# Two matmul layers of a dense FFN, dealt out in turns on TensorE: a quarter of the next unit's first layer, then one token tile of this unit's second layer

## The reference

```
x = x + L0_xattn(layernorm(x), ctx)
x = x + L0_ffn(layernorm(x))          # 8 experts, 2 per token
x = x + L1_xattn(layernorm(x), ctx)
x = x + L1_ffn(layernorm(x))          # 64 experts of 64, 8 per token, and 2 shared MLPs of 512
```

```
probs = softmax(xf @ router_w + router_b); tw, ti = top_k(probs, 8); tw = tw / sum(tw)
for e in range(64):
    h = silu(xf @ W1[e] + B1[e]) @ W2[e] + B2[e]
    acc = acc + (sum of tw where ti == e)[:, None] * h
shared = sum over 2 of (silu(xf @ SW1 + SB1) @ SW2 + SB2)
out = acc + shared
```

## Time and profile before

| | |
|---|---|
| time, median of 3 runs | 1457.45 us (1457.34 to 1457.92) |
| profiled execution: its time, its span | 1458.33 us, 1456.6 us |
| PE busy | 1396.3 us (96%) |
| PE weight loads busy | 1115.3 us (77%) |
| DVE busy | 1011.6 us (69%) |
| ACT busy | 779.7 us (54%) |
| POOL busy | 288.1 us (20%) |
| mean granted TensorE clock | 0.989 |
| stage D | from about 992 us to the end |

### The profile page before, as it was taken

How to read it: one execution, slowest core, us unless ns; L and a number is a source line. 1 busy time by engine, 2 the same in 40 slices (tenths; PEclk the granted TensorE clock), 3 DMA queues, 4 the chain that set the end, 5 groups by cost and what they waited for, 6 DMA issues and landing times.

```text
span 1456.6 us, 27434 instructions
## 1 busy us (share of the span) xinstructions
PE 1396.3 (96%) x9946; PEld 1115.3 (77%) x9946; DVE 1011.6 (69%) x2461; ACT 779.7 (54%) x1682; POOL 288.1 (20%) x329
## 2 busy tenths in 40 slices
PE   6999998998999979999999999999999999999998
PEld 5898997885556656666667666767899999999997
DVE  6767773565656668977877787776587776677753
ACT  4556663344766657777878777772443222222221
POOL 0000001243155232300000000002233332233321
PEclk9999999999999999999999999999999999999999
DMA  9432201423455111100000000001036544555441
GB/s 345 148 110 68 77 22 30 146 80 117 153 185 182 58 52 31 38 13 2 16 23 20 13 30 2 2 2 64 0 92 150 121 116 103 127 118 123 99 104 52
DMA packets 78479, 117.80 MB, mean 81 GB/s; under 512 B 7487, under 2 KB 51845, under 8 KB 77829
## 3 DMA queue, kind: packets, MB, share of 16 engines
q1 hardware_dynamic: 75269, 107.59, 25.7%
q0 software_dynamic: 3072, 8.39, 1.8%
HBM read 97.09 MB, written 18.87 MB: 80 GB/s over the span
## 4 chain that ended last, share of the span: by engine, by line
PE 81%; DVE 10%; issue 3%; ACT 3%; POOL 2%; DMA 1%; SPq 0%; ACTq 0%; DVEq 0%; POOLq 0%
PE PS L68 17%; PE PS L70 16%; PE PS L69 16%; PE PS L2602 7%; PE PS L2574 6%; PE PS L1292 5%; PE PS L2589 3%; PE PS L2617 3%; PE PS L1308 2%; PE PS L1186 2%; DVE a_pt L838 2%; DVE c_sm L2826 1%; POOL zs L1506 1%; DVE a_c L754 1%; ACT c_pr L2698 1%
## 5 line engine op out<-in xcount | busy, mean ns | idle before, releaser
L1842 ACT ACTIVATE d_hf<-PS,C 128x512 f32<-128x512 f32 x160 | 108.7, 691 | 255.0 <-PE PS L70 252.3
L953 POOL CAST d_h<-d_hf 128x512 fp32r<-128x512 f32 x160 | 126.2, 802 | 329.1 <-DVE d_hf L2050 248.3
L2707 ACT ACTIVATE c_pt<-PS 100x512 f32<-100x512 f32 x256 | 139.0, 595 | 93.7 <-PE PS L2589 93.5
L68 PE MATMUL PS<-d_w,d_h 128*128 128x256 f32 x640 | 182.2, 285 | 2.0 <-issue 1.4
L70 PE MATMUL PS<-d_w,d_h 128*128 128x256 f32 x640 | 179.8, 281 | 0.0
L69 PE MATMUL PS<-d_w,d_h 128*128 128x256 f32 x640 | 179.7, 281 | 0.0
L2698 ACT ACTIVATE c_pr<-c_sm,c_mn 128x400 f32<-128x400 f32 x256 | 158.7, 626 | 14.5 <-DVE c_mn L2826 14.5
L2826 DVE CUSTOM_DVE_ANT_0 c_sm<-PS,c_mw 128x400 f32<-128x400 f32 x256 | 136.0, 569 | 16.9 <-PE PS L2574 14.9
L958 DVE TENSOR_TENSOR d_h<-d_hf,d_h 128x512 fp32r<-128x512 f32 x160 | 129.7, 868 | 16.2 <-POOL d_h L953 13.2
L2050 DVE TENSOR_TENSOR d_hf<-d_hf,d_wb 128x512 f32<-128x512 f32 x128 | 89.8, 709 | 71.0 <-ACT d_hf L1842 70.6
L68 PE MATMUL PS<-ZT,d_w 128*128 128x512 f32 x320 | 126.1, 394 | 0.7 <-issue 0.7
(11 more groups left out here) (305 smaller groups left out, 3128.6 us busy)
## 6 DMA issues: line engine op xcount, KB each, us to landing
d_wb<-wscratch SPq DMA_DIRECT2D x64, 512.0 KB, 7.3
a_cT<-ctxT SPq DMA_DIRECT2D x4, 1601.0 KB, 7.7
a_raw_nat<-ctx SPq DMA_DIRECT2D x4, 1536.0 KB
zs<-e_zero SPq DMA_DIRECT2D x2, 2944.0 KB, 18.6
ys<-e_y SPq DMA_DIRECT2D x46, 128.0 KB, 1.8
d_w1r<-l_w SPq DMA_DIRECT2D x10, 512.0 KB, 4.0
d_w2r<-l_w SPq DMA_DIRECT2D x10, 512.0 KB, 5.2
e_z<-zs SPq DMA_DIRECT2D x9, 512.0 KB, 3.9
```

The costliest lines, as they stand in the source:

```text
L68: pe.matmul(out, w[0], x[0], start=first, stop=False)
L953: i = eng.tensor_copy(mem["h"][b % 2][0][:, m, :], mem["hf"][:, m, :])
L1842: act.activation(memD["hf"][:, m, :], PS[:, m, :], ACT.Silu, bias=C[:, b1 + m:b1 + m + 1]).then_inc(DM["act"], 1)
L2707: act.activation(c_pt[u % 2][0:KW, :, :, i * P + r * DH:i * P + (r + 1) * DH].rearrange("p h t q -> p (h t) q"), PS[0:KW, BT + r, :].rearr ...
```

## The change

Two code pieces change, both in `d_pe`. `second` now takes one tile `i`; its waits for `h_lo` and the rest stand ahead of tile 0, and its wait for `x_done` is halved: tile 0 waits for the first addition of the unit before (bank 4), tile 2 for the second (bank 5). The loop deals out quarters and tiles in turns. Nothing else of the program differs, and the number of instructions is the same.

```diff
-            def second(u):
+            def second(u, i):
                 g, b = u // B, u % B
-                pe.wait_ge(DM["h_lo"], u * 4 + 4)
...
-                wait_past(pe, x_done[3], u * 2)
...
+                if i == 0:
+                    pe.wait_ge(DM["h_lo"], u * 4 + 4)
...
+                if i % 2 == 0:
+                    wait_past(pe, x_done[3], (u - 1) * 2 + i // 2 + 1)
+                o = PS[:, 4 + i // 2, (i % 2) * D:(i % 2 + 1) * D]
+                for k in range(4):
+                    last = split_matmul(pe, o, [h[:, k, i * P:(i + 1) * P] for h in memD["h"][b % 2]],
+                                        [w[:, k, :] for w in memD["w2"][g % 2]], k == 0, k == 3 and g < GD - 1)
...
+                if i == QT - 1:
+                    last.then_inc(DM["y"], 1)
...
             for u in range(DU):
                 if u + 1 < DU:
-                    d_hidden(pe, u + 1)
-                second(u)
+                    d_hidden(pe, u + 1, [0])
+                for i in range(QT):
+                    second(u, i)
+                    if i + 1 < QT and u + 1 < DU:
+                        d_hidden(pe, u + 1, [i + 1])
```

More of the change, by code:

```diff
@@ L1881, in d_pe @@
         def d_pe(pe):
-            def second(u):
+            def second(u, i):
                 g, b = u // B, u % B
-                pe.wait_ge(DM["h_lo"], u * 4 + 4)
-                if u == 0:
-                    pe.wait_ge(DM["w_lo"], 2)
-                    pe.wait_ge(attn_done, 1)
-                wait_past(pe, x_done[3], u * 2)
-                if g == GD - 1:
[L1890 to L1900, removed]
+                if i == 0:
+                    pe.wait_ge(DM["h_lo"], u * 4 + 4)
+                    if u == 0:
+                        pe.wait_ge(DM["w_lo"], 2)
+                        pe.wait_ge(attn_done, 1)
+                    if g == GD - 1:
+                        pe.wait_ge(DR["one"], B)
+                        pe.wait_ge(DR["wt_out"], b + 1)
+                        pe.wait_ge(DR["w_in"], 64)
+                if i % 2 == 0:
[4 more added lines that the diff above has]
+                                        [w[:, k, :] for w in memD["w2"][g % 2]], k == 0, k == 3 and g < GD - 1)
+                if g == GD - 1:
+                    last = pe.matmul(o, d_wT[b][:, i * P:(i + 1) * P], d_b2[:, :], start=False, stop=True)
+                if i == QT - 1:
+                    last.then_inc(DM["y"], 1)
             def logits(b):
```

## The result

The change makes the kernel slower by 7%: 1559.06 us (median of 4, 1556.56 to 1561.84) against 1457.68 us (median of 4), ratio 1.0704, 95% interval 1.0691 to 1.0718, or 101.4 us. The prediction was 1568 us, with a range of 1538 to 1597. The kernel before took 1457.5 us in some groups of runs and 1489 to 1493 us in others, so each experiment is told by its distance from the kernel before of its own group; one run of the third experiment, over 1.5% above the fastest of its kernel, is left out of its figures.

What follows compares the result with a forecast made beforehand. TensorE was taken to bound stage D. Waits of 81.3 us, 85.4 with the opening, plus 25 us of clock falls made 110 us on the profiled 1458.33; less 0.9 for the median, 1568 us, range 1538 to 1597.

Steps and rivals of the forecast that it cites:

- What bounds the kernel: Stage D: TensorE sets the time, busy 244.40 of 244.40 us, with idle spots of only 0.55 and 1.43 us.
- The wait for the low parts: Ahead of tile 0 in each unit: a chain of 5.18 us against a cover of 2.78, so TensorE 2.4 us late.
- Units that round weights: Seven of units 8 to 36: low parts take 3.75 instead of 2.90 us beside GpSimd's cast, late by 3.25 us.
- Units 0 to 7: First units, without a multiply: 3.05 us against a cover of 2.78 plus router matmuls; nothing taken, bound 2 us.
- Opening: Start of stage D: three quarters of unit 1 no longer fill the wait for unit 0's low parts, 4.1 us lost.
- End: Last group: units 37 and 38 late by 2.0 us each, unit 39 by 3.3, net 1.7.
- Sum of the waits: Units 8 to 39 lose 81.3 us in waits, 85.4 us with the opening.
- Matmuls in turns: Borders between quarters and tiles on TensorE: cost and gain nil, bound 0.1 us per unit, 4 us in all.
- The clock: TensorE's clock behind the new pauses: 16 falls to the lower level at 1.56 us each, 25 us.
- at this length it is even odds: New pauses, some 2.15 us idle: the clock falls behind half of them, judged from six earlier stretches.
- the rival of 1544 us: Clock holds at pauses of 2.15 us and falls at the opening alone: 1544 us, chance 0.22.
- the upper one: Clock falls at nearly every pause, or the chain is longer than priced: 1591 us or above 1597, chance 0.17.

Runs made afterwards that it cites:

- the third experiment: The change, but tile 0 waits for both additions of the unit before, as in the kernel before: 1643.23 us against 1492.53 for the kernel before.
- the fifth experiment: The change, with GpSimd's cast of the next group's second-layer weights put between its casts of quarters 0 and 1: 1579.63 us against 1488.86 for the kernel before.
- the second run: The change itself measured once more, unaltered, in another group of runs: 1591.86 us against 1488.86 for the kernel before, ratio 1.0681.
- the sixth experiment: The change, with nine unread matmuls of 512 columns ahead of tile 0 in units 12 to 35: 1585.99 us against 1488.86 for the kernel before.

## Why the prediction was right

- **What bounds the kernel** stood: TensorE waited for nothing in D, and with the cover restored (8.5, 5.5 us) or turns limited to units 0 to 7 (6.0 us) it is back near the old time. No gain from turns was found.
- **The wait for the low parts**: 2.4 us late per unit was forecast, shown as a pause of 2.15; it is 2.22, and the period 13.62 (forecast 13.5). The parts of the chain were tested apart: low parts behind the fourth multiply (2.22 to 1.20 when two are moved away), the addition (2.22 to 2.81 with a second one), the cover (2.22 to nothing with 5.56 us), and that the pause has a fixed end (filled for nothing).
- **Units that round weights**: 3.06 us for a forecast of 3.0, in the six from 13 to 33; unit 9 has 2.62 and unit 8 1.78, since router matmuls stand in the cover, which I counted for units 0 to 7 and not for these (read from the code's order; no run moved them). That it is GpSimd's cast was shown by the fifth experiment.
- **Units 0 to 7**: nil, as taken. **Opening**: the 4.04 us pause against 0.55 before, 3.5 for a forecast of 4.1. **End**: 1.78 for units 37 and 38, 3.17 for unit 39 against 1.43, net 1.74 for a forecast of 1.7.
- **Sum of the waits**: 85.4 us forecast; 78.1 shown and 8 hidden are 86.
- **Matmuls in turns**: nil was taken. The period of 13.62 us is the 11.12 of before, the pause of 2.22 with 0.26 for its start and end, and 0.02 left over.
- **The clock** is the term that was off. Sixteen falls at 1.56 us were forecast, 25 us; there were nine, 14 us (the price of one held: periods with a fall are 15.19 us, those without 13.62). That is the 11 us by which the forecast lies too high; the other terms came out 2 us low in sum. The step that failed is "at this length it is even odds", from six pauses, for all pauses from 2 us alike. For those of 3.06 us it held (three of six, four of six in the second run), for those of 2.22 it did not: one of 21 and two of 21, where half had been forecast. The six rows were not all there was either: the same trace has falls behind pauses of 1.40 us (clock 0.76 from 412.88 to 420.00 us) and 1.89 us (0.65 from 525.11 to 533.00).
- **Length alone** doesn't settle it. Time at half clock went up with the pauses: 12 us with 1.20, 13 with 2.22 alone, 32 with 2.22 and 3.06, 95 with 2.81 and 3.65. But the two pauses of 1.78 us in units 37 and 38 had a fall each in both runs of the change, where the same length in unit 8 had none. Why these are hit stays open.
- The Trainium skill (TensorE: Matmul & The Clock Gate, "Why this matters for your kernels") advises against idle gaps over some 3 us between bursts of matmuls. To take shorter ones as harmless, as the rival of 1544 us did, doesn't hold here: the clock fell behind 13 of 21 pauses of 2.81 us in the third experiment, and that rival did not come.
- **The rivals**: the upper one, a fall at nearly every pause, is what the third experiment's 2.81 us came nearest to; the change did not.

## What to carry to other kernels

Before dealing out two phases finer on the bounding engine, count what stands between the last producer's piece and the first consumer's piece: if the consumer needs all pieces, fine turns shrink that cover (here from 11.1 to 2.8 us) while the chain over the other engines (5.2 us) stays. Running two pieces ahead instead of one restored it here. A wait that was free because it came late (`x_done`, here) has to be counted again in each new order. So has the clock behind each new pause: here pauses of 2.22 us cost little of it, those of 3.06 a fall in every second, and pauses that nothing can shorten may be filled with unread matmuls, as in the sixth experiment.

## What the runs showed of the hardware that I had not expected

- Half-clock time grows steeply with the pause, some 30 pauses each: 13 us where the ordinary ones and those of units that round weights are all 2.22, 32 us where six of them are 3.06, 95 us at 2.81 and 3.65. With 24 pauses filled with matmuls the clock did not fall there at all.
- An instruction of one engine put "ahead" of its neighbours on an idle queue runs when the queue gets to it: GpSimd's cast moved by program order stayed beside the same low parts.
- GpSimd's cast of 1024 columns takes 1.04 us alone and 1.50 beside VectorE's low parts, and these take 3.75 instead of 2.90 us.
